# State space stage of a twelve-stage decoder: the first step-width chain moved into the stage ahead, the gate moved to VectorE

## The reference

```
z, xBC, dt = x @ W_in                     # 4096, 4352 and 64 columns
xBC = silu(causal convolution, 4 taps, of xBC)      # 4096 columns of x, 128 of B, 128 of C
dt  = softplus(dt + dt_bias)              # 64 heads; max(dt,0) + log1p(exp(-|dt|))
decay = exp(-exp(A) * dt)                 # per head and token
h_t = decay_t * h_(t-1) + dt_t * x_t B_t ;  y_t = C_t h_t + D * x_t
y = y * silu(z);  y = y * rsqrt(mean(y^2) + 1e-5) * norm_weight
out = layernorm(x + y @ W_out)
```

## Time and profile before

| | us |
|---|---|
| median of three runs | 4168.1 |
| lowest and highest | 4166.07, 4176.48 |
| the profiled execution | 4173.8 |
| its span | 4172.0 |
| busy PE / DVE / ACT / POOL, whole span | 3614.6 / 2960.1 / 1925.4 / 1481.8 |

### The profile page before, as it was taken

The page is one execution under the profiler, slowest core; times in us unless marked ns, Lnnn a source line. Parts: engine busy times, 40 slices in busy tenths (PEclk is TensorE's granted clock), DMA queues, the critical chain, the costliest instruction groups (busy, mean ns, idle before and its releaser), DMA issues.

```text
span 4172.0 us, 65936 instructions
## 1 busy us (share of the span) xinstructions
PE 3614.6 (87%) x23748; PEld 2230.1 (53%) x23762; DVE 2960.1 (71%) x6387; ACT 1925.4 (46%) x4723; POOL 1481.8 (36%) x1336
## 2 busy tenths in 40 slices
PE   7799999998981868789999979879989999997885
PEld 3466666665651436644555555555555555554544
DVE  7799989988659674533555658857777777775678
ACT  4466666665532324312333324435545555553345
POOL 2533213333302000000111123017979888895220
PEclk9899999999985989989999989899999999997887
DMA  2222222222200100020000000302211112121000
GB/s 70 64 70 67 55 65 66 65 64 50 50 14 30 34 23 2 2 75 22 1 1 1 1 31 2 126 8 79 76 61 72 71 66 71 66 72 68 1 1 21
DMA packets 240578, 185.94 MB, mean 45 GB/s; under 512 B 117632, under 2 KB 216576, under 8 KB 239168
## 3 DMA queue, kind: packets, MB, share of 16 engines
q1 hardware_dynamic: 240256, 181.73, 14.4%
HBM read 166.45 MB, written 15.20 MB: 44 GB/s over the span
## 4 chain that ended last, share of the span: by engine, by line
PE 43%; DVE 22%; issue 16%; POOL 13%; ACT 4%; SPq 1%; DMA 1%; POOLq 0%; DVEq 0%; ACTq 0%
PE ps L310 10%; POOL mE L3365 7%; POOL mSQ L3376 4%; PE ps L2161 3%; PE ps L2886 3%; PE ps L2899 3%; PE ps L2865 2%; PE ps L502 2%; PE ps L2196 1%; PE ps L2679 1%; PE ps L580 1%; PE ps L1972 1%; DVE hMX L2954 1%; PE ps L316 1%; ACT lP L2260 1%
## 5 line engine op out<-in xcount | busy, mean ns | idle before, releaser
L310 PE MATMUL ps<-xT,min 128*128 128x512 f32 (+1 forms) x1072 | 499.1, 612 | 8.4 <-DVE macc L3307 7.7
L3307 DVE SCALAR_TENSOR_TENSOR macc<-ps,mcw,macc 128x508 f32<-128x508 f32 (+2 forms) x408 | 302.9, 742 | 183.6 <-ACT macc L3242 173.9
L3369 POOL TENSOR_TENSOR macc<-macc,mZ 128x512 f32<-128x512 f32 x128 | 384.8, 3006 | 70.3 <-DVE macc L3320 65.5
L3365 POOL TENSOR_TENSOR mE<-mE,mCB 128x1024 f32<-128x1024 f32 x128 | 307.9, 2407 | 18.0 <-ACT mCB L3253 15.8
L310 PEld LDWEIGHTS ps<-xT,min 128*128 128x128 f32 (+1 forms) x1072 | 191.8, 191 | 227.1 <-issue 210.8
L3181 PE MATMUL ps<-mwo,macc 128*128 128x256 f32 x1024 | 261.7, 400 | 42.4 <-POOL macc L3369 37.6
L3317 DVE TENSOR_TENSOR_SCAN mE<-mE,mid 128x1024 f32<-128x1024 f32 x128 | 295.1, 2306 | 0.0
L2351 POOL TENSOR_TENSOR lP<-lP,lm 128x512 f32<-128x512 f32 x64 | 66.6, 1041 | 574.5 <-DVE lm L2324 574.5
L826 POOL TENSOR_TENSOR dTB<-did,dNB 128x1024 f32<-128x1024 f32 (+1 forms) x10 | 29.3, 2928 | 661.7 <-DMA dNB<-d_N 597.6
L2924 ACT ACTIVATE hE<-ps 128x512 f32<-128x512 f32 x256 | 139.0, 594 | 222.2 <-PE ps L2886 222.2
L3181 PEld LDWEIGHTS ps<-mwo,macc 128*128 128x128 f32 x1024 | 188.3, 194 | 93.9 <-POOL macc L3369 72.2
(11 more groups left out here) (573 smaller groups left out, 8605.7 us busy)
## 6 DMA issues: line engine op xcount, KB each, us to landing
mE<-m_decay SPq DMA_DIRECT2D x128, 512.0 KB, 3.6
dwk<-in_L_attn_Wk SPq DMA_DIRECT2D x64, 128.0 KB, 2.3
dwq<-in_L_attn_Wq SPq DMA_DIRECT2D x64, 128.0 KB, 2.3
...
d_N<-dNT SPq DMA_DIRECT2D x256, 16.0 KB, 1.5
```

Source lines behind the costliest of these rows:

```text
L310: t = pe.matmul(out, w[:, j, :], self.c.xT[:, j, blk(g, 512)], start=j == 0, stop=j == 1)
L3307: x = dve.scalar_tensor_tensor(out=acc[:, :, 3 - j:T], in0=p[:, :, 0:T - 3 + j], scalar=self.cw[:, i, j:j + 1], in1=acc[:, :, 3 - j:T], op ...
L3365: pool.tensor_tensor(E, E, bc(self.CB[g % 2][:, :, :].rearrange("p b t -> p (b t)"), 2), ALU.mult).then_inc(*self.em.up)
L3369: pool.tensor_tensor(self.acc[s][:, :], self.acc[s][:, :], self.Z[s][:, :], ALU.mult).then_inc(*self.ys.up)
```

## The change

Five edits, all in `Ternary` and `Scan`:

1. The first step-width half (product, abs, relu, exp, ln, ten chain steps, decays) is issued in rounds 12 to 16 of the ternary stage (table `ASIDE`), by `tensor_step`, `scalar_step` and `vector_step`. Its four buffers are the last eight blocks of `mwo`, which are loaded later. SP stores the decays before it waits for the ternary stage.
2. The second half, with the turn of token group 3, is spread over rounds 2 to 20 (table `LATE`). The reciprocal is cut in four pieces.
3. The gate goes from GpSimd to VectorE: the skip term is written to bank 7, and the product with `mZ` reads it there. Bank 7 is free after the gate and not after the skip term.
4. The square stands between `z` and `x` instead of behind `tr`; the group's end is spread over rounds t-4 to t-12, and the last scaling goes to ScalarE as scale and offset.
5. GpSimd scales 24 blocks of `mwo` in the ternary stage and eight in rounds 17 to 22.

```diff
# Ternary
+    ASIDE = {12: (("dt", 0),), 13: (("exp", 0),), 14: (("ln", 0), ("chain", 0)), 15: tuple(("chain", k) for k in range(1, 7)),
+             16: tuple(("chain", k) for k in range(7, 10)) + (("decays", 0),)}
...
+            for step, k in self.ASIDE.get(t, ()):
+                yield "aside", step, k
# Scan
+    LATE = {2: ("turn", 1), 3: ("dt", 1), 4: ("exp", 1), 6: ("chain", 0), 7: ("ln", 1), 8: ("chain", 1), 9: ("chain", 2), 10: ("chain", 3),
...
-        for t in range(len(seq) + 8):
-            for step, q in (("yd", t - 3), ("x2", t - 1), ("em", t - 1), ("z", t), ("x", t), ("close", t - 4), ("cb", t - 1), ("decay", t),
-                            ("tr", t - 1), ("taps", t), ("sq", t - 3), ("acc", t - 3), ("y", t - 2), ("sums", t - 4), ("stats", t - 5),
-                            ("rsqrt", t - 6), ("scale", t - 7)):
+        for t in range(len(seq) + 13):
+            for step, q in (("yd", t - 3), ("x2", t - 1), ("em", t - 1), ("z", t), ("sq", t - 3), ("x", t), ("close", t - 4), ("cb", t - 1),
+                            ("decay", t), ("rsq", t - 5), ("sums", t - 7), ("stats", t - 9), ("rsqrt", t - 11), ("scale", t - 12),
+                            ("tr", t - 1), ("taps", t), ("acc", t - 3), ("y", t - 2)):
...
-                room[7] = self.yd.at(u + 1)
+                room[7] = self.ys.at(u + 1)
...
-                dve.scalar_tensor_tensor(out=self.acc[s][:, :], in0=self.acc[s][:, :], scalar=self.s[:, 34 + i:35 + i], in1=bank(7),
+                dve.scalar_tensor_tensor(out=bank(7), in0=self.acc[s][:, :], scalar=self.s[:, 34 + i:35 + i], in1=bank(7),
                                          op0=ALU.mult, op1=ALU.add).then_inc(*self.yd.up)
+                dve.wait_ge(*self.zt.at(u + 1))
+                dve.wait_ge(*self.yd.at(u + 1))
+                dve.tensor_tensor(self.acc[s][:, :], bank(7), self.Z[s][:, :], ALU.mult).then_inc(*self.ys.up)
...
-            elif step == "yd":
-                pool.wait_ge(*self.yd.at(u + 1))
-                pool.wait_ge(*self.zt.at(u + 1))
-                pool.tensor_tensor(self.acc[s][:, :], self.acc[s][:, :], self.Z[s][:, :], ALU.mult).then_inc(*self.ys.up)
...
+            elif step == "scale":
+                act.wait_ge(*self.off.at(g + 1))
+                for j in range(4):
+                    x = act.activation(c.X[:, 4 * g + j, :], c.R[:, j, :], ACT.Identity, scale=c.rsq[:, j:j + 1], bias=c.rsq[:, 12 + j:13 + j])
+                x.then_inc(*c.xn.up)
```

More of the change, by code:

```diff
@@ L2643, in tensor @@
         for step, u, h in self.order():
+            if step == "aside":
+                self.next.tensor_step(pe, u, h)
+                continue
             g, b = divmod(u, 4)
@@ L2692, in scalar @@
         for step, u, h in self.order():
+            if step == "aside":
+                self.next.scalar_step(act, u, h)
+                continue
             g, b = divmod(u, 4)
@@ L2755, in vector @@
         for step, u, h in self.order():
+            if step == "aside":
+                self.next.vector_step(dve, own, u, h)
+                continue
             g, b = divmod(u, 4)
@@ L3105, in order @@
                         yield step, q, units[q], g, i
-                elif step in ("close", "sums", "stats", "rsqrt", "scale"):
+                elif step in ("close", "rsq", "sums", "stats", "rsqrt", "scale"):
                     if i == 31:
@@ L3132, in tensor @@
             s, to = q % 4, 4 * (g % 2)
-            if step == "parts":
+            if step == "turn":
+                c.turn_tensor(pe, self.n - 1, 3, (4, 5))
+            elif step == "dt":
+                self.tensor_step(pe, step, 1)
+            elif step == "parts":
                 x = self.chain[q][0]
@@ L3226, in scalar @@
                 act.copy(to, bank(4).rearrange("p (j e h) -> p j e h", j=4, e=2)).then_inc(*self.cols.up)
-            elif step == "chain":
-                if q == 1:
-                    decay(1)
+            elif step == "turn":
+                c.turn_scalar(act, self.n - 1, 3, (4, 5))
+            elif step in ("dt", "exp", "ln", "decays"):
+                self.scalar_step(act, step, 1)
+            elif step == "scale":
[3 more added lines that the diff above has]
+                x.then_inc(*c.xn.up)
             elif step == "z":
@@ L3267, in scalar, with vector_step, chain_step, then @@
                 act.activation(self.tn[s][:, :], self.acc[s][:, :], ACT.Square).then_inc(*self.sq.up)
+    def vector_step(self, dve, own, step, k):
+        if step == "chain":
+            self.chain_step(dve, own, 0, k)
+    def chain_step(self, dve, own, n, k):
+        x, e, u, d = self.chain[n]
+        def then(ins):
+            dve.wait_ge(own.sem, own(ins))
+        if k == 0:
+            dve.wait_ge(*self.e0.at(n + 1))
+            then(dve.tensor_scalar(d, e, 1.0, 1.0, ALU.add, ALU.subtract))
+        elif k == 1:
+            dve.wait_ge(*self.ln.at(n + 1))
+            then(dve.scalar_tensor_tensor(out=u, in0=d, scalar=0.0, in1=u, op0=ALU.is_equal, op1=ALU.max))
+        elif k == 2:
+            then(dve.scalar_tensor_tensor(out=d, in0=d, scalar=0.0, in1=d, op0=ALU.is_equal, op1=ALU.add))
+        elif k < 7:
+            then(dve.reciprocal(d[:, blk(k - 3)], d[:, blk(k - 3)]))
+        elif k == 7:
+            then(dve.tensor_tensor(d, d, e, ALU.mult))
+        elif k == 8:
+            then(dve.tensor_tensor(d, d, u, ALU.mult))
+        else:
+            dve.wait_ge(*self.rel.at(n + 1))
+            dve.memset(g4(u)[:, :, 0:1], 0.0)
+            dve.tensor_tensor(x, x, d, ALU.add).then_inc(*self.dtx.up)
     def vector(self, dve, own):
@@ L3301, in vector @@
             if step == "chain":
-                chain(1, q)
+                self.chain_step(dve, own, 1, q)
             elif step == "taps":
@@ L3324, in vector @@
                 dve.tensor_scalar(self.sw[:, 4:8], bank(6)[:, 0:4], 1.0 / 4096, 1e-5, ALU.mult, ALU.add).then_inc(*self.smv.up)
+            elif step == "rsq":
+                dve.wait_ge(*self.smv.at(g + 1))
+                last = c.rsqrt_rest(dve, own, [self.sw[:, blk(n, 4)] for n in range(3)])
             elif step == "sums":
                 sw = self.sw
-                dve.wait_ge(*self.smv.at(g + 1))
-                r = c.rsqrt_rest(dve, own, [sw[:, blk(n, 4)] for n in range(3)])
+                if g:
+                    dve.wait_ge(*c.xn.at(4 * self.n + g))
                 dve.wait_ge(*self.accd.at(u + 1))
-                dve.wait_ge(own.sem, r)
+                dve.wait_ge(own.sem, last)
                 for j in range(4):
@@ L3360, in gpsimd @@
                 pool.memset(self.SQ[g % 2][:, :], 0.0).then_inc(*self.sq0.up)
+            elif step == "wo":
+                if q == 0:
+                    pool.wait_ge(self.dma[10], 16)
+                for i in (24 + 2 * q, 25 + 2 * q):
+                    w = scaled(i)
+                if q == 3:
+                    w.then_inc(*self.won.up)
             elif step == "em":
```

163 lines of the change are left out of this document (76 added, 87 removed).

## The result

The changed kernel takes 4106.17 us (median, 4106.13 to 4119.67) against 4167.09 (4161.99 to 4176.48) for the kernel before: ratio 0.9858, 95% interval 0.9842 to 0.9874. It is faster by 60.9 us, 1.4%. The forecast was 4094 with a range of 4080 to 4126: the time lies in the range, 12 us above the value and at the upper end of the forecast's own 4083 to 4106.

A forecast was written before the change was run, and what follows sets the result against it. A loop through turn, square, gate and output product was taken to close the round, leaving TensorE as bound. Start 17.2, rounds and group ends 55.8, end 1.4 sum to 74.4 us off 4173.8; median 5.7 lower: 4094, range 4080 to 4126.

The forecast's parts named there:

- The start: From the ternary stage's last normalization to the seventh tap group: first chain hidden in ternary rounds, 17.2 us won.
- T1 to T7: First to seventh of the state space stage's 136 tap groups: 37.0 us instead of 38.1, bounds 33 and 42.
- The gate: Gate product on VectorE with one input in PSUM: 0.71 us, instead of 3.19 on GpSimd.
- The round: Steady state space round, skip term to skip term: 6.90 us instead of 7.13, 28.3 us won over 123 rounds.
- The group ends: Three group ends and six passes without a unit, in the state space stage: 27.5 us won.
- clock 1.00 through a group's end: Sign of being right: granted clock stays at 1.00 through a group's end, where it was 0.91.
- an idle TensorE of several us at a group's end: Sign of being wrong: TensorE waits several us at a group's end.
- The end: Last three rounds and last scaling: 1.6 us won, 0.2 lost, net 1.4 us.
- The group ends stay: Rival: rsqrt pieces and GpSimd block each other, TensorE drops to half rate; 27.5 us lost, 4121 us, chance 0.13.
- The round stays: Rival: another loop closes the steady round at the same 7.13 us; 28.3 us lost, 4122 us, chance 0.12.
- the start wins nothing: Rival: ternary rounds or table loads cost what the gap before the first tap group gave; 4111 us, chance 0.12.
- The cover of the scan: Slower rival: VectorE's scan meets GpSimd's decay product holding the port every round; 160 us more, 4254 us, chance 0.05.

The follow-up runs named there:

- e1: The kernel before with the gate alone moved from GpSimd to VectorE, skip term in bank 7: 4120.33 us, ratio 0.989.
- e8: The changed kernel with the first step-width chain taken out of the ternary stage and run whole at the state space stage's head: 4116.16 us, ratio 0.9866.
- e7: The changed kernel with GpSimd's square sum and decay product cut to 4 columns beside the group ends' reciprocal square roots (output wrong): 4087.45 us, ratio 0.9799.
- e3: The changed kernel with both reciprocal square root pieces of a group's end placed behind the taps of their round: 4089.74 us, ratio 0.981.
- e2: The changed kernel with the gate back on GpSimd and all else as changed: 4213.46 us, ratio 1.0108.

## Why the prediction held, and where it was off

**The start.** 17.2 forecast, 16.0 measured (T7 stands 15.9 earlier): right. T1 to T7 was put at 37.0 and took 36.8. The ternary stage's price for its guest was put at 2.9 and was 4.3, with a scatter of some 3 us in that stage's own code (e1 against before). The table switches ran as the trace had said: the exponential's load at 2765.77 took 1.28 us and its activation started at 2767.07. What I had not seen is how the gain splits: e8 gives the first chain 6.2; the rest came with the other edits, the spreading of the second chain above all, which no run takes back alone.

**The gate and the round.** The gate was put at 0.71 and takes 0.69. The round was put at 6.90, read from two turns at a place where I took TensorE to be free of waits; it is 6.82, in the changed kernel and in e1. 0.31 x 123 is 38 us where 28.3 stood. The output product measures 1.89 us without a wait, 1.99 with one, and in the turn of the earlier trace rows it was 1.96, which is most of the 0.08.

**GpSimd.** Busy time fell from 1481.8 to 1167.6 us, 314 instead of 380: the square sum moved next to the scan, and its mean rose from 1.28 to 1.88.

**The group ends: the failed step.** Beside its 123 rounds T7 to T136 held 56.4 us; the forecast made 28.9 of them, and 53.3 were measured. So nearly the whole of its 27.5 us by the ends did not come. The forecast added "2.5 a group for the rsqrt pieces" and held that "a tap group may be some 2 us late before TensorE feels it". Per group 3.5 us over nine rounds of 6.90 were forecast (2.5, and 1.0 of the 1.8 for the two products), and 9.4, 11.3 and 11.3 over nine of 6.82 measured: 21.4 us too few. Even the bounds of 0 to 6 us a group for the rsqrt pieces were too low: without the mean's product, 1.26, there remain 8.1, 10.0 and 10.0. The forecast had counted two or three blocked instructions in a row, but priced each by the 1.12 of the earlier trace rows, which is the rest of an instruction of GpSimd; the second of the two that block waits out a whole decay product, 2.27. This happens once per root and so twice a group, and I spent one margin of 2 us on blocks of 1.0 + 2.1 us plus nine steps of 0.2. e7 shows that the blocks are GpSimd's, e3 that the place ahead of the taps makes them TensorE's. Of the prediction's signs, "clock 1.00 through a group's end" failed (0.97) and "an idle TensorE of several us at a group's end", a sign of being wrong, came.

**The sum.** T7 to T136: 21.4 more for the ends, 9.8 less for the rounds (0.08 x 123), some 2.6 more for the passes beside the B-C projections (33.3 us for four spacings; 27.3 + 3.5 + 1.6 = 32.4 by the forecast's terms), and 0.4 more for the second chain's rounds (T7 to T29 takes 3.4 us over 22 rounds where 3.0 stood): the 14.6 us. Together with 1.2 of the start that is 15.8 in the profile. The end was put at 1.4 and gained 2.1 (T136 to the last scaling 29.3 us, then 27.2). Between the medians the miss is 12.2.

That the value is this close is partly luck: the round, mis-sized the other way, took back 9.8 of the 24.4 us that the ends and passes missed. Without it the same ends give some 4116 us, still in the range of 4080 to 4126, which had been made wide enough for the ends to fail, but outside the forecast's own 4083 to 4106.

**The rivals.** "The group ends stay" was nearly the case: 31.9 us of excess instead of 34.9, 24.4 of its 27.5 us lost, and by the cause it named: rsqrt pieces and GpSimd block each other, and a product behind a wait runs slower (3.38 us for 1.98). It would have given 4121 by its price, and the shorter round made part of that good. "The round stays" and "the start wins nothing" did not come. The cover of the scan, the rival on the slow side, did not come: the scan stays at 2.28 in the steady round. e2 shows a loop that I had not listed: gate, square, x bias, taps, skip term, gate. The order closes it, and in the changed kernel it costs nothing only because the gate is fast.
